# A gated cross-attention kernel: the second batch's last full context group is loaded in blocks and turned by VectorE, and the hand-written orders of all engines are redrawn

## What is computed

```python
scores = jnp.einsum('bsd,bmd->bsm', layernorm(x), ctx) / sqrt(D)
scores = jnp.where(mask[:, None, :], scores, -1e30)
x = x + tanh(g_xattn[0]) * einsum('bsm,bmd->bsd', softmax(scores), ctx)   # 0 where no row is valid
ff = qdot(gelu(qdot(layernorm(x), w_gating[0])) * qdot(layernorm(x), w_gating[1]), w_linear)  # fp8 e4m3
return x + tanh(g_ffn[0]) * ff
```

## Time and profile before

| | us |
|---|---|
| median of 3 runs | 126.36 |
| the three runs | 126.28, 127.42, 126.36 |
| the profiled execution, its own time | 127.25 |
| its span (first to last instruction of the core) | 125.5 |
| TensorE matmuls busy in the span | 120.9 |
| VectorE / ScalarE / GpSimd busy | 97.0 / 87.8 / 82.3 |

### The profile page before, as it was taken

How to read it: one execution, slowest core, us unless ns; L and a number is a source line. 1 busy time by engine, 2 the same in 40 slices (tenths; PEclk the granted TensorE clock), 3 DMA queues, 4 the chain that set the end, 5 groups by cost and what they waited for, 6 DMA issues and landing times.

```text
span 125.5 us, 2568 instructions
## 1 busy us (share of the span) xinstructions
PE 120.9 (96%) x863; PEld 104.2 (83%) x863; DVE 97.0 (77%) x210; ACT 87.8 (70%) x155; POOL 82.3 (66%) x143
## 2 busy tenths in 40 slices
...
PEclk9999999999999999999999999999999999999999
DMA  3958994678986899769997000510000000001133
GB/s 99 320 189 334 416 290 49 94 123 229 264 291 102 159 218 130 110 81 284 356 254 102 0 0 0 130 45 0 0 0 5 0 0 0 3 0 47 42 125 125
DMA packets 34440, 15.73 MB, mean 125 GB/s; under 512 B 26230, under 2 KB 33019, under 8 KB 34427
## 3 DMA queue, kind: packets, MB, share of 16 engines
...
...
## 4 chain that ended last, share of the span: by engine, by line
PE 66%; SPq 11%; DMA 10%; ACT 4%; issue 4%; DVE 3%; DVEq 0%; ACTq 0%
PE ring L774 13%; SPq L369 10%; DMA cn<-in_ctx_dram 8%; PE scores L854 6%; PE pv L825 6%; PE pv L833 6%; PE pv L829 6%; PE scores L788 6%; PE scores L791 6%; PE scores L792 6%; PE ring L870 6%; DMA raw<-in_ctx_dram 2%; ACT gate L575 2%; DVE ring L639 1%; PE scores L808 1%
## 5 line engine op out<-in xcount | busy, mean ns | idle before, releaser
L461 POOL TENSOR_TENSOR chl<-cn,chl 128x256 fp32r<-128x256 f32 (+1 forms) x52 | 37.8, 761 | 7.1 <-ACT chl L519 7.0
L645 DVE TENSOR_TENSOR pT_lo<-ring,pT_hi 128x512 fp32r<-128x512 f32 (+1 forms) x32 | 17.6, 578 | 6.9 <-ACT pT_hi L512 6.7
L512 ACT ACTIVATE pT_hi<-ring 128x512 fp32r<-128x512 f32 (+1 forms) x32 | 15.6, 513 | 8.3 <-PE ring L774 8.1
L645 DVE TENSOR_TENSOR cT_lo<-ring,cT_hi 128x512 fp32r<-128x512 f32 (+1 forms) x28 | 16.8, 624 | 4.5 <-ACT cT_hi L512 4.5
L792 PE MATMUL scores<-cT_hi,xT_lo 128*128 128x512 f32 (+2 forms) x60 | 20.1, 342 | 0.0
L791 PE MATMUL scores<-cT_lo,xT_hi 128*128 128x512 f32 (+2 forms) x60 | 20.0, 342 | 0.0
L469 POOL TENSOR_TENSOR ws<-ws,wc 128x256 f32<-128x256 f32 x24 | 15.4, 674 | 6.0 <-DVE wc L687 6.0
L825 PE MATMUL pv<-chl,pT_hi 128*128 128x256 f32 (+1 forms) x104 | 18.9, 294 | 0.0
L512 ACT ACTIVATE cT_hi<-ring 128x512 fp32r<-128x512 f32 (+1 forms) x28 | 14.6, 547 | 5.3 <-PE ring L774 3.2
L833 PE MATMUL pv<-chl,pT_lo 128*128 128x256 f32 (+1 forms) x104 | 17.5, 281 | 0.0
L829 PE MATMUL pv<-chl,pT_hi 128*128 128x256 f32 (+1 forms) x104 | 17.5, 280 | 0.0
...
## 6 DMA issues: line engine op xcount, KB each, us to landing
...
raw<-in_ctx_dram SPq DMA_DIRECT2D x24, 64.0 KB, 2.5
act<-in_ctx_dram SPq DMA_DIRECT2D x24, 64.0 KB, 2.9
...
```

The costliest lines, as they stand in the source:

```text
L461: last = nc.gpsimd.tensor_tensor(chl[b % 2][0:parts, t, D:2 * D], cn[b % 2][0:parts, t, :], chl[b % 2][0:parts, t, 0:D].bitcast(f32), ALU. ...
L512: nc.scalar.activation(dst, bank_view(f, size), ACT.Copy).then_inc(hi_ready, 1)
L645: nc.vector.tensor_tensor(dst, bank_view(f, size), hi.bitcast(f32), ALU.subtract).then_inc(lo_ready, 1)
```

## The change

TensorE no longer transposes C1:4 and C1:5. A seventh block load T1:2 is put into the SP queue, and VectorE gets the steps D1:5 and D1:4. With that, batch 1 falls into by_block too: its three full groups are loaded in 1 KB pieces, and its mask row is read in another order. All six order strings are redrawn. The only line of code that changes makes G3 wait for the same load of x as G2 does, since G3 now comes first. The diff, cut to one line of each order that shows the new steps:

```diff
     PE_ORDER = """
-        C1:0 C0:6 S0:1 S0:2 X1 S0:3 C1:3 C1:2 S1:2 S1:3 C1:5 S2:0 P0:1 P0:0 S2:1 P0:2 C1:6 S3:0 S3:1 C1:4
+        B0:3 C1:0 X1 S0:2 S0:3 C1:2 C1:1 S1:2 C1:3 S1:3 S2:0 C1:6 S2:1 P0:1 P0:0 S3:0 S3:1 P0:2 P1:3 V0:0
...
     DVE_ORDER = """
-        G2 M1:1 C1:5 P0:1 G3 P0:2 P0:0 M2:0 D2:1 C1:6 C1:4 C2:1 W1 P1:0 M3:0 D2:0 P0:3 P1:1 C2:0 A0 P1:3
+        C1:3 D1:5 M1:1 C1:6 G2 C1:5 P0:1 P0:0 D1:4 M2:0 C1:4 P1:3 P0:2 W1 P1:1 P0:3 P1:2 D2:0 D2:1 P1:0 A0
...
     SP_ORDER = """
-        X1 C1:0 W0 M1 C1:1 C1:2 X2 C1:3 T2:0 T2:1 W1 W2 M3 C2:0 C2:1 T2:2 W3 M2 C3:3 C2:3 T3:0 T3:1 C3:0
-        C2:2 C3:1 C3:2 W4 T3:2 W5"""
+        X1 C1:0 W0 M1 X2 C1:1 C1:3 T1:2 M2 C1:2 C2:0 W1 T2:0 C2:2 C2:1 C2:3 T2:1 T2:2 W2 T3:0 C3:3 W3 C3:2
+        M3 C3:0 T3:1 W4 C3:1 T3:2 W5"""
...
                     else:
-                        if s[1] < 3:
-                            dve.wait_ge(x_in[s[1] - 1], 16)
+                        dve.wait_ge(x_in[min(s[1], 2) - 1], 16)
                         stats(s[1])
```

More of the change, by code:

```diff
@@ L62, in gated_cross_attention_ffn @@
-        P5:2 S7:1 S7:2 N0 V5:0 P5:3 P6:1 V5:1 S7:3 N1 P6:0 P6:2 V5:2 V5:3 P6:3 H0 V6:0 V6:1 P7:0 P7:1 V6:2
-        V6:3 H1 P7:3 V7:0 P7:2 V7:1 V7:2 V7:3 H2 N2 H3 H4 H5 H6 N3 H7 H8 H9 H10 H11 Y0 H12 Y1 H13 H14 H15 Y2
-        Y3 Y4 Y5 Y6 Y7"""
-    ACT_ORDER = """
[L68 to L73, removed]
@@ L76, in gated_cross_attention_ffn @@
-    DVE_ORDER = """
-        G0:0 G0:1 X0:0 C0:0 X0:1 C0:1 C0:2 C0:3 G1 C0:4 C0:5 M1:0 W0 C1:1 C1:0 C0:6 M0:0 M0:1 X1 C1:3 C1:2
-        G2 M1:1 C1:5 P0:1 G3 P0:2 P0:0 M2:0 D2:1 C1:6 C1:4 C2:1 W1 P1:0 M3:0 D2:0 P0:3 P1:1 C2:0 A0 P1:3
[L79 to L83, removed]
+        X0:0 C0:0 W2 X0:1 C0:1 W3 A1:0 A0:0 W3 C0:2 C0:3 A0:1 A1:1 B0:0 C0:5 C0:4 B0:1 S1:1 B0:2 C0:6 S0:1
@@ new lines, in gated_cross_attention_ffn @@
+        B0:3 C1:0 X1 S0:2 S0:3 C1:2 C1:1 S1:2 C1:3 S1:3 S2:0 C1:6 S2:1 P0:1 P0:0 S3:0 S3:1 P0:2 P1:3 V0:0
+        S2:2 P1:1 P0:3 P1:2 V0:1 P1:0 V0:2 V0:3 S2:3 X2 V1:0 V1:1 V1:2 P2:1 S3:2 S3:3 P2:2 S5:0 S5:1 P2:3
+        S4:0 V1:3 P2:0 P3:1 S4:1 V2:0 C2:6 P3:0 V2:1 P3:2 S4:2 S4:3 V2:2 V2:3 P3:3 S5:2 V3:0 V3:1 V3:2 X3
+        V3:3 S5:3 P4:1 P4:0 P4:2 S6:0 S6:1 V4:0 C3:6 V4:1 V4:2 S6:2 P4:3 S6:3 P5:1 P5:0 S7:0 N0 S7:1 P5:2
+        V4:3 S7:2 P6:0 V5:0 V5:1 P5:3 P6:2 S7:3 N1 V5:2 V5:3 H0 P6:1 V6:0 P6:3 P7:0 P7:1 V6:1 V6:2 P7:3 V6:3
@@ new lines, in gated_cross_attention_ffn @@
+        P7:2 H1 V7:0 V7:1 V7:2 V7:3 H2 N2 H3 H4 H5 H6 N3 H7 H8 H9 H10 H11 Y0 H12 H13 H14 Y1 H15 Y2 Y3 Y4 Y5
+        Y6 Y7"""
+    ACT_ORDER = """
+        X0:0 C0:0 X0:1 C0:1 R0:0 C0:2 C0:3 R0:2 B0:0 C0:5 C0:4 B0:1 R0:3 K1 C0:6 B0:2 R0:1 C1:0 X1 B0:3 B1
+        C1:1 C1:2 C1:3 E0 C1:6 C1:5 P0:1 P0:0 E1 R1:3 C1:4 P1:3 P0:2 R1:2 P1:1 P0:3 P1:2 K2 P1:0 C2:0 C2:1
+        R1:0 R1:1 X2 E2 C2:2 P2:1 C2:3 P2:2 C2:4 E3 P2:3 P2:0 C2:5 P3:1 B2 R2:3 C2:6 R2:1 P3:0 R2:2 P3:2
+        C3:0 R2:0 P3:3 E4 C3:3 C3:2 K3 C3:1 X3 R3:3 R3:2 P4:1 P4:0 P4:2 R3:1 B3 C3:6 C3:4 C3:5 E5 P4:3 L0
+        R3:0 P5:0 P5:1 E6 P6:0 P5:2 N0 L1 P5:3 P6:2 N1 E7 P6:1 H0 P7:0 P6:3 P7:2 P7:1 P7:3 H1 L2 H2 N2 H3 H4
+        L3 H5 H6 N3 H7 H8 H9 H10 H11 H12 H13 H14 H15"""
@@ new lines, in gated_cross_attention_ffn @@
+    DVE_ORDER = """
+        G0:0 G0:1 X0:0 C0:0 X0:1 C0:1 C0:2 C0:3 G1 C0:5 C0:4 M1:0 C0:6 W0 M0:0 C1:0 M0:1 X1 G3 C1:1 C1:2
+        C1:3 D1:5 M1:1 C1:6 G2 C1:5 P0:1 P0:0 D1:4 M2:0 C1:4 P1:3 P0:2 W1 P1:1 P0:3 P1:2 D2:0 D2:1 P1:0 A0
+        M2:1 C2:0 M3:0 C2:1 X2 D2:2 D2:3 C2:2 P2:1 C2:3 D2:4 M3:1 P2:2 C2:4 W2 P2:3 D2:5 A1 P2:0 U0 C2:5
+        P3:1 M5:0 C2:6 M4:0 D3:0 P3:0 M4:1 A2 P3:2 C3:0 D3:3 D3:2 P3:3 C3:3 D3:1 C3:2 C3:1 X3 U1 A3 P4:1
+        P4:0 M5:1 P4:2 D3:5 D3:4 W3 C3:4 C3:5 C3:6 M6:0 U3 P4:3 M6:1 U2 P5:1 P5:0 A4 M7:0 U4 P5:2 P6:0 M7:1
+        P5:3 A5 P6:2 P6:1 W4 P6:3 U5 P7:0 H0 A6 P7:3 P7:1 U6 P7:2 H1 W5 A7 U7 H2 H3 H4 H5 H6 H7 H8 H9 H10
+        H11 H12 Y0 Y1 H13 H14 Y2 H15 Y3 Y4 Y5 Y6 Y7"""
```

16 lines of the change are left out of this document (6 added, 10 removed).

## The result

| | before | after |
|---|---|---|
| median, us (runs) | 126.41 (4) | 131.91 (4) |
| lowest to highest | 126.28 to 127.42 | 131.05 to 132.71 |
| profiled execution / its span | 127.25 / 125.5 | 131.05 / 129.3 |
| ratio of the times, 95% interval | | 1.043 [1.038, 1.048] |

Where executions of a kernel lie more than 1.5% above its fastest, a ratio leaves them out and a median does not, so a ratio can be smaller than the quotient of two medians.

A forecast was written before the change was run, and what follows sets the result against it. TensorE was taken as the bound, with VectorE and the loads close behind in the first half. Fills 0.88, idle matmul 0.11 and hole 0.39, less wait 0.25, gave 1.13 us off 126.36: 125.2 us, range 124.2 to 127.5.

The forecast's parts named there:

- Two fills, 0.88 us: TensorE loses two fills of four transposes, each 0.44 us in the chain: 0.88 us gained.
- third rival: Transposes were hidden anyway; the saved time reappears as a wait at the next late thing: 126.1 us, chance 0.10.
- price of some 0.27 us a transpose: TensorE's transposes do not overlap, so two fills are worth 2.2 us: 123.9 us, chance 0.02.
- T1:2 and D1:5, wait 0.25: VectorE's turn D1:5 waits for block load T1:2, wanted by 24.6 and expected at 24.4: 0.25 us lost.
- free DMA time 7.0 us ... so 4.21 fits in the sum: Between 16 and 64 us the DMA engines have 7.0 us free, so an added block load of 4.21 us fits.
- first rival: The new load decides: T1:2 late, later block loads behind their turns; 129.2 us at full size, 127.5 half hidden; chance 0.22.
- The hole of 0.39 at 64.15: TensorE's hole from batch 2's late context load goes, as the SP order issues that context before T2:1: 0.39 us gained.
- The redraw at nothing: All engines' redrawn orders: no cost of their own was counted.
- fourth rival: The redraw does more than counted: T1:2 in time, ScalarE's 0.86 us partly on the path; 124.6 us, chance 0.14.
- VectorE's turns at nothing: VectorE's two added turns, 1.26 us in all, fit in its 4.1 us idle from 16 to 64 us: counted at nothing.
- second rival: VectorE becomes the bound between 16 and 64 us; 1.26 us added, 1.38 gained: 126.2 us, no change; chance 0.12.
- ScalarE's bias at nothing: ScalarE's batch 1 bias row falls from 1.73 and 1.02 us to 1.16 and 0.73, 0.86 less, counted at nothing.

The follow-up runs named there:

- turns only: Changed kernel with reordered SP loads and fo's edit, without T1:2; D1:5 and D1:4 turn rows already in cn (keys wrong): 126.16 us, 0.999 of the kernel before.
- load only: Changed kernel with reordered SP loads and fo's edit, TensorE transposing C1:5 and C1:4, T1:2's 512 KB loaded unread behind C1:2: 127.83 us, 1.009 of the kernel before.
- load with turns: Changed kernel with reordered SP loads (T3:1 directly behind T3:0) and fo's edit, T1:2 and both VectorE turns kept: 129.58 us, 1.018 of the kernel before.

## Why the prediction was wrong

- **Two fills, 0.88 us.** Right in mechanism, and in size within 0.1 to 1.2 us: turns against transposes, with no load between them, differ by 0.89 us in the medians and 0.7 by the ratios. So the third rival (the transposes were hidden) is out, and so is a price of some 0.27 us a transpose, 2.2 in all.
- **T1:2 and D1:5, wait 0.25.** P0:1 was forecast at 25.8 and stands at 25.54; D1:5 runs at 23.66 without a wait, inside the "no wait" bound. The term is 0, and the working for it holds. It was the wrong place to look.
- **The failing step: "free DMA time 7.0 us ... so 4.21 fits in the sum".** An average share over 48 us was set against the cost of an undisturbed load. The queue is in order, and 4.21 us is about the least that a block load held it for in any trace; T1:2 took 9.65 and T2:0 10.08. The prediction's own rows had one of 12.03. The deadline of the new load was worked out, those of the loads behind it were not: W1, T2:1 and T3:2 came 0.99, 2.33 and 1.10 us late, and these make 0.94 + 1.73 + 0.53 = 3.2 us of TensorE's 4.9. This is the first rival's mechanism, "every later block load may come behind its turn". But its turning point was tied to T1:2 being late by 1.1 us, and the rest of the line was late with T1:2 in time; so its chance of 0.22 was too low for a reason that the text names itself. Its price, 129.2 at full size, was too low as well.
- **The hole of 0.39 at 64.15 is gone.** Right in itself: ScalarE reads cn at 60.69 without a wait. But the context loads of batch 2 that were moved ahead of T2:1 for it (C2:0, C2:2, C2:1 and the tail C2:3) are part of the traffic behind which W1 and T2:1 came late, and another hole of 1.46 us opened at 64.42.
- **The redraw at nothing: a second failed step.** The prediction has no cost for the redrawn orders, and its fourth rival even a gain. 129.21 us without any seventh load says that they cost 2.9 us by themselves. With another order of the load queue and fo's edit, and every other order as it was, 0.5 of these are left (1.004). How the 2.4 divide between the load order and fo was not tried apart, and the holes of that trace (1.30 and 0.21 us) show only about half of the 2.9; fo is worth 1.8 us in the changed kernel and was not named in the prediction. The two failed steps do not add up: the load costs 4.3% in the old orders, the redraw 2.4% without the load, and both together 4.3%.
- **VectorE's turns at nothing.** Right, and so the second rival was not what happened: turns only gives 0.999, and VectorE is less busy than before between 36 and 64 us.
- **ScalarE's bias at nothing.** 1.16 and 0.73 as forecast (18.64 and 19.68 us), and with the layout alone no gain is seen (1.001).
- **The sum, 1.13.** Even with no seventh load the best version found is level with the kernel before (0.999 [0.996, 1.002]). So in the orders tried there was nothing to win that can be measured against the kernel before, and the loss came on top.

What stays open is the step between load only (0.7 us by the ratios) and load with turns (2.5 us). It does not look like the two buffers (with a third T3:2 is as late) nor like VectorE's time (turns only is free). In the version with both, T1:2 also stands one context load further ahead than in load only, since its turn needs it by 24 us. That C1:2 and what follows are pushed back by it fits the rows, where the loads just ahead of T3:2 go out some 1.8 us later than with the load only, but it wasn't tried alone.
